# Values and gate products of two batches moved to other slots, and the causal mask of some maxima moved from VectorE to TensorE

## The reference

```python
qkv = (x @ w_qkv).reshape(b, s, 3, HEADS, HEAD_DIM)
q, k, v = (qkv[:, :, 0], qkv[:, :, 1], qkv[:, :, 2]); q = q / scale
scores = jnp.where(causal_mask, einsum('bqhd,bkhd->bhqk', q, k), NEG)
x = layernorm(x + einsum('bhqk,bkhd->bqhd', softmax(scores), v).reshape(b, s, HIDDEN) @ w_out)
weights, experts = top_k(softmax(x @ gate), 4); weights = weights / weights.sum(-1)
y = sum over the 4 experts of weight * (u * silu(g)) @ down,  with g, u = split(x @ gate_up)
out = layernorm(x + y)
```

## Time and profile before

| | before |
|---|---|
| median of 3 runs | 429.66 us (426.7 to 431.03) |
| the profiled execution: its time, its span | 431.4 us, 429.4 us |
| mean granted clock of PE | 0.964 of 2.4 GHz |
| busy over the span | PE 378.1, DVE 289.5, ACT 242.5, POOL 235.9 us |
| busy in pairs 14 to 16 (28.68 us) | PE 27.27, DVE 18.84 us |
| busy in pairs 17 to 21 (29.50 us) | PE 22.89, DVE 26.23 us |
| busy in pairs 25 to 28 (27.87 us) | PE 22.65, DVE 23.86 us |

### The profile page before, as it was taken

The page is one execution under the profiler, slowest core; times in us unless marked ns, Lnnn a source line. Parts: engine busy times, 40 slices in busy tenths (PEclk is TensorE's granted clock), DMA queues, the critical chain, the costliest instruction groups (busy, mean ns, idle before and its releaser), DMA issues.

```text
span 429.4 us, 10419 instructions
## 1 busy us (share of the span) xinstructions
PE 378.1 (88%) x2826; PEld 217.2 (51%) x2826; DVE 289.5 (67%) x1159; ACT 242.5 (56%) x534; POOL 235.9 (55%) x374
## 2 busy tenths in 40 slices
PE   5979899999996799877998999997999999989880
PEld 2526554445543356433354455665676777655340
DVE  1167868885499885989789759864656666544453
ACT  2431657765545586535766628654666656546942
POOL 5321245434232585625782672777777777646872
PEclk9999999999999899968899999999999999999966
DMA  4858554755563275393727463665665656338693
GB/s 132 266 194 223 181 179 140 223 136 161 156 197 87 52 233 162 99 275 78 227 73 230 148 172 87 179 178 172 189 176 154 173 172 177 104 83 326 264 382 129
DMA packets 54071, 74.77 MB, mean 174 GB/s; under 512 B 9842, under 2 KB 45308, under 8 KB 52480
## 3 DMA queue, kind: packets, MB, share of 16 engines
q1 hardware_dynamic: 46832, 56.93, 46.6%
q0 software_dynamic: 6912, 16.93, 10.7%
q10 hardware_dynamic: 272, 0.26, 0.2%
HBM read 46.33 MB, written 29.66 MB: 177 GB/s over the span
## 4 chain that ended last, share of the span: by engine, by line
PE 44%; DVE 18%; SPq 16%; issue 10%; DMA 5%; ACT 3%; POOL 3%; ACTq 0%; DVEq 0%; POOLq 0%
SPq L507 13%; PE PS L854 8%; PE PS L814 6%; PE PS L783 5%; PE PS L833 5%; PE PS L797 3%; DVE WOT L1412 3%; DVE junk L1412 3%; PE PS L690 3%; SPq L489 3%; PE PS L914 2%; PE PS L712 2%; POOL scratch_slots L1753 2%; PE PS L884 2%; PE PS L739 2%
## 5 line engine op out<-in xcount | busy, mean ns | idle before, releaser
L1125 ACT ACTIVATE PT<-PS 128x512 f32<-128x512 f32 x160 | 92.0, 596 | 51.5 <-PE PS L833 47.0
L1762 POOL DMA_INDIRECT scratch_y<-Y,XG x80 | 79.8, 997 | 34.0 <-issue 18.0
L1734 POOL TENSOR_SCALAR_AFFINE_SELECT PT<-PT 128x256 f32<-128x256 f32 (+1 forms) x140 | 50.2, 367 | 77.2 <-ACT PT L1125 75.9
L1753 POOL DMA_INDIRECT scratch_slots<-XP,RI x64 | 64.0, 1000 | 40.7 <-DVE XP L1354 20.6
L814 PE MATMUL PS<-KS,QS 96*128 96x512 bf16 (+3 forms) x256 | 63.7, 310 | 19.0 <-DVE MX L1412 18.3
L1412 DVE CUSTOM_DVE_ANT_0 junk<-PS,mneg 128x512 bf16<-128x512 f32 (+3 forms) x128 | 58.4, 483 | 22.3 <-PE PS L814 22.2
L833 PE MATMUL PS<-QS,KS 98*128 98x512 bf16 (+3 forms) x256 | 63.0, 308 | 1.2 <-ACT PT L1125 0.9
L690 PE MATMUL PS<-W,XGT 128*64 x320 | 60.5, 332 | 1.1 <-DVE WG L1275 0.6
L692 PE MATMUL PS<-WG,XGT 128*64 128x192 f32 x320 | 60.6, 332 | 0.0
L1412 DVE CUSTOM_DVE_ANT_0 WOT<-PS,mneg 128x512 bf16<-128x512 f32 (+3 forms) x96 | 43.9, 484 | 9.0 <-PE PS L814 9.0
L814 PEld LDWEIGHTS PS<-KS,QS 96*128 96x128 bf16 x256 | 21.7, 100 | 55.4 <-DVE MX L1412 43.8
(11 more groups left out here) (233 smaller groups left out, 658.1 us busy)
## 6 DMA issues: line engine op xcount, KB each, us to landing
XG<-scratch_slots SPq DMA_DIRECT2D x160, 65.0 KB, 2.6
scratch_qk<-PA SPq DMA_DIRECT2D x14, 384.0 KB, 3.1
W<-in_gate_up_dram SPq DMA_DIRECT2D x16, 288.0 KB, 3.7
KS<-scratch_qk SPq DMA_DIRECT2D x32, 128.0 KB, 3.8
YL<-scratch_y SPq DMA_DIRECT2D x8, 512.0 KB, 6.6
QS<-scratch_qk SPq DMA_DIRECT2D x8, 384.0 KB, 4.1
QS<-scratch_qk SPq DMA_DIRECT2D x24, 128.0 KB, 3.9
W<-in_down_dram SPq DMA_DIRECT2D x8, 288.0 KB, 4.8
```

The lines of the kernel that those rows point to most:

```text
L1125: e.activation(PT[:, p % NPT, n, :], PS[:, 2 + (rank[u] - 1) % 2, :], ACT.Exp).then_inc(st_exp, 1)
L1734: e.affine_select(out=d, in_=d, compare_op=ALU.is_ge, fill=0.0, base=0, pattern=[[0, 1 if n < 2 else 2], [1, 128]], channel_multiplier=-1) ...
L1753: e.indirect_dma_start(out=XS[:, :], out_offset=bass.IndirectOffsetOnAxis(ap=RI[:, b % 2, TOPK * q + n:TOPK * q + n + 1], axis=0), in_=XP[ ...
L1762: e.indirect_dma_start(out=YK[:, :], out_offset=bass.IndirectOffsetOnAxis(ap=XG[:, j % NXG, D + 1:D + 2].bitcast(I32), axis=0), in_=Y[:, j ...
```

## The change

`v` and `xg` of batch 2 move from slots 70 to 74 to slots 85 to 90, `v` and `xg` of batch 3 from slots 110 to 114 to 126 to 131. The last two `qk` of batch 3 move from slots 74 and 77 to 98 and 102, so that `load` 7, which reads what they make, is still behind them. `att` and `proj` of batch 0 then come one to four slots earlier. The weights of experts 6 to 14 move from slots 120 to 130 to slots 134 to 140, behind the `xg` that they wait for. Second, PE masks by a product (L828 of the changed kernel) in unit 4 of all 32 pairs, and in all five units of pairs 17 to 21 and 24 to 27; there DVE takes the maximum by `tensor_reduce`, in unit 4 by one instruction for both heads.

```diff
-WEIGHTS = ((0, 3, 75), (3, 3, 80), (6, 3, 120), (9, 3, 125), (12, 3, 130), (15, 4, 142), (19, 3, 145), (22, 3, 160),
+WEIGHTS = ((0, 3, 75), (3, 3, 80), (6, 3, 134), (9, 3, 137), (12, 3, 140), (15, 4, 143), (19, 3, 145), (22, 3, 160),
            (25, 3, 163), (28, 4, 165))
...
+VALUES_AT = (85, 126)
+VECTOR_FULL = (*range(17, 22), *range(24, 28))
...
             for c in range(2 if b > 1 else 0):
-                put(5 * (8 * b - 2) + 2 * c, ("v", b, c))
+                put(VALUES_AT[b - 2] + 2 * c, ("v", b, c))
...
             for n, m in enumerate((0, 2, 1, 3) if b > 1 else ()):
-                put(first + 4 * n + 5, ("qk", b, m))
+                put(98 + 4 * n - 8 if b == B - 1 and n >= 2 else first + 4 * n + 5, ("qk", b, m))
...
     for b in range(1, B):
-        put(5 * (8 * b - 2) + 4, ("xg", b))
+        put(5 * (8 * b - 2) + 4 if b == 1 else VALUES_AT[b - 2] + 5, ("xg", b))
...
+def mask_by_product(i, n):
+
+    return n == 4 or i in VECTOR_FULL
...
                         t = e.matmul(PS[:, kk, c0:c0 + w], QS[r][0:96, h, 128 * qt:128 * qt + 128],
-                                     KS[r][0:96, h, 0:w], start=(c0 == 0), stop=True, skip_group_check=True)
+                                     KS[r][0:96, h, 0:w], start=(c0 == 0), stop=not mask_by_product(i, n),
+                                     skip_group_check=True)
+                    if mask_by_product(i, n):
+                        wait_const(e, "idb")
+                        last = PS[:, kk, :].rearrange("p (a c) -> p a c", c=128)
+                        last = last[:, 3:4, :] if n < 2 else (last[:, 2:4, :] if n < 4 else last[:, 1:4:2, :])
+                        t = e.matmul(last, idb[:, :], mneg[:, S - 128:S].unsqueeze(1).broadcast_to(last.shape),
+                                     start=False, stop=True, skip_group_check=True)
...
-                    for h, qt, c0 in pair_scores(n, h0, 3, 2, 1):
+                    if n == 4:
+                        t = e.tensor_reduce(M[:, h0:h0 + 2, 1], PS[:, kk, :].rearrange("p (h n) -> p h n", h=2),
+                                            AX.X, ALU.max)
+                    for h, qt, c0 in pair_scores(n, h0, 3, 2, 1) if n < 4 else ():
                         w = 128 * (qt + 1)
-                        t = e.tensor_tensor_reduce(sums_of(i, kk)[:, c0:c0 + w], PS[:, kk, c0:c0 + w], mneg[:, S - w:S],
-                                                   1.0, LOWEST, ALU.add, ALU.max, M[:, h, qt:qt + 1])
+                        if mask_by_product(i, n):
+                            t = e.tensor_reduce(M[:, h, qt:qt + 1], PS[:, kk, c0:c0 + w], AX.X, ALU.max)
+                        else:
+                            t = e.tensor_tensor_reduce(sums_of(i, kk)[:, c0:c0 + w], PS[:, kk, c0:c0 + w],
+                                                       mneg[:, S - w:S], 1.0, LOWEST, ALU.add, ALU.max,
+                                                       M[:, h, qt:qt + 1])
```

## The result

The changed kernel took 422.5 us in the median of its four runs (422.1 to 425.5), the kernel before 428.7 (426.7 to 431.0); the ratio is 0.9848, 95% interval [0.9801, 0.9894], about 6 us. The profiled execution took 422.5 us, its span is 420.8; that of before took 431.4, its span 429.4.

What follows compares the result with a forecast made beforehand. PE was taken to bound pairs 14 to 16 and 22, DVE 17 to 21 and 25 to 28. Terms -8.9 - 4.9 + 4.8 + 0.3 + 0.3 = -8.4 us gave 421.3 us for the median, range 414.5 to 428.5.

Steps and rivals of the forecast that it cites:

- What bounds: In the maxima, PE bounds pairs 14 to 16 and 22, DVE bounds pairs 17 to 21 and 25 to 28.
- the 8.9 us in pairs 14 to 16: Two halves of `v`, one `xg` and two `qk` leave these PE-bound pairs, and all their time comes back: -8.9 us.
- Pair 22: Batch 3's `v` and `xg`, 5.47 us, leave it; it ends at 4.5 us, a gain of 4.9.
- floor of the quiet pairs: Pairs 8 to 11 take 4.43 us each, the least a pair was taken to need.
- The cover: PE's idle time hides moved work: 4.6 of 6.61 us in pairs 17 to 21, 3.6 of 5.22 in 25 to 28.
- The rival that blocks don't fit: Moved blocks on PE let DVE run dry and cost full length in both routing stretches: +7.1 us, 436.8; 11 in 100.
- The masks: PE pays 0.44 us per fully masked pair, 2.2 in pairs 17 to 21; DVE gains 0.07 per unit 4.
- The clock: Time at 1.2 GHz given back once PE is full: 1.7 us in pairs 17 to 21, 3.4 in 25 to 28.
- Behind the maxima: What follows the maxima is untouched and moves with their end: 0 us.
- the chances: Faster than 425.4 us: 0.52 from the main case, 0.09 full gain, half of 0.22 for POOL and weights, given as 0.71.
- POOL: POOL becomes the bound in pairs 19 to 22 and 27 to 31, making `pv` wait: +4 us, 425; 14 in 100.
- The backlog of the weights: Weights of experts 6 to 14 delay the maxima's small transfers, needed in pair 30: +3 us, 424; 8 in 100.

Runs made afterwards that it cites:

- b_again1: The kernel before, unchanged, profiled a second time; 431.1 us in one run.
- e6_batch2: The kernel before with only the moves of batch 2's `v` and `xg` and batch 3's last two `qk`, all masks on DVE; 425.3 us, ratio to before 0.9882.
- e9_halves: The changed kernel with only unit 4's masks on PE and each moved half of `v` cut in two pieces, one slot between; 422.7 us, ratio to before 0.9846.
- e10_moves_again: The changed kernel's new order with no mask on PE, all masks on DVE, run a second time; 422.0 us, ratio to before 0.9822.
- e5_batch3: The kernel before with only the moves of batch 3's `v` and `xg` and the weights behind them, all masks on DVE; 424.9 us, ratio to before 0.9899.
- e2_masks: The changed kernel with the order put back to that of before, so only the masks change; 428.7 us, ratio to before 1.0022.
- e4_fused_dve: The changed kernel, but DVE keeps the fused masked operation in units 0 to 3 of the nine fully masked pairs; 423.9 us, ratio to before 0.9888.
- e1_moves: The changed kernel's new order with all masks left on DVE, none on PE; 423.2 us, ratio to before 0.988.
- e8_weights_late: The changed kernel with the weights of experts 6 to 21 put later still, slots 143 to 158 instead of 134 to 145; 423.4 us, ratio to before 0.985.

## Why the prediction was right, and where its terms were not

**What bounds** was read rightly: PE in pairs 14 to 16 and 22, DVE in 17 to 21 and 25 to 28. In the first two nearly all the work taken out came back. Of the 8.9 us in pairs 14 to 16, 0.7 stayed: the shorter stretch has a wait of PE for DVE of 1.0 us, now that DVE has 17.90 us of work in 20.44. Pair 22 stopped at 4.90, 0.5 above the floor of the quiet pairs.

**The cover** was larger than forecast. I let 4.6 of 6.6 us of idle time in pairs 17 to 21 serve; with moves and masks 5.3 of 6.4 us of waits went, and the 1.4 us that PE is idle now are 0.3 a pair, between the 0.4 that I took off and the 0.2 of the quiet pairs. The moves alone cost 4.1 us there (b_again1 against e6_batch2), so 4.8 of their 8.9 were covered. The rival that blocks don't fit is refuted by that, and by the 1.1 us of waits left; e9_halves says that the length of a piece doesn't matter in pairs 17 to 21.

**The masks** were priced at 2.2 us for pairs 17 to 21. By the difference to e10_moves_again they cost 32.77 - 32.09 = 0.7, by doubling them 1.05. The step that failed is the one that took PE's time for a mask as the stretch's, though PE has waits into which part of it falls: I had filled the cover with the moved work and left none for the masks. That the plain reduction is no dearer than the fused one held: 0.598 against 0.611 us, while the Trainium skill ("VectorE: DVE Perf Modes", "Rules for kernel authors") calls `tensor_reduce` the slowest operation of DVE; no run here bears that out for a maximum over PSUM. Unit 4's gain is 0.09 where I had 0.07.

**The clock** was about right in size and wrong as a gain. I took 5.1 us as given back. Of the forecast for pairs 17 to 21 that is 1.7, and the first and second profile of before differ by 1.55 there: right in size, but the stretch was not there in the second profile, so it is no gain over a usual run.

For pairs 25 to 28 I reckoned half of each low microsecond as lost and one stretch of two as given back, 3.4 us. Between before and e6_batch2, the same order there with 13.7 and 3.4 us of low clock, lie 2.2 us: 0.22 per low microsecond, and not 0.5. That DVE bounds there and PE had room would explain it, but no run takes this apart, and in pairs 17 to 21, where DVE bounds too, the 3.4 us cost 0.46 each. Both stretches were gone, which by 0.22 is 3.0 us: two errors that nearly cancel, so the clock doesn't explain why the difference was -1.5 us and not +0.3. The rest does. Moves less cover and masks were to add 5.5 + 1.8 - 3.6 = 3.7 us; from the 24.9 that the old order would take by this estimate without a low clock, the changed kernel's 26.38 is 1.5 more. Of that the moves alone are 0.8 (e5_batch3), and the masks, which cost nothing there in the old order (24.18 in e2_masks), the other 0.7. So here too moved work and masks were priced too high, not the clock.

**Behind the maxima** I had nothing, and 2.2 us went. PE waits there for tiles of rows from memory in both kernels (the bracket: idle before it, and for what), in the changed one

```profile
284.51 0.41 PE L665 MATMUL PS<-idf,XG 128*128 128x128 f32 x2 [1.71 <-DMA XG<-scratch_slots]
285.85 0.69 PE L665 MATMUL PS<-idf,XG 128*128 128x128 f32 x2 [0.92 <-DMA XG<-scratch_slots]
```

and in the one before

```profile
295.77 0.41 PE L658 MATMUL PS<-idf,XG 128*128 128x128 f32 x2 [1.64 <-DMA XG<-scratch_slots]
296.92 0.43 PE L658 MATMUL PS<-idf,XG 128*128 128x128 f32 x2 [0.74 <-DMA XG<-scratch_slots]
```

but in the changed kernel the clock then fell for 6.8 us:

```profile
285.30:292.10 6.80, 6.25 (x32) 4.09 (x33) 2.16 (x5) 1.51 (x5) 5.28 (x6) 0.50 0.65 205
```

and in the one before it didn't. From the first product of round 9 to that of round 12 are 15.2 us with that and 12.3 without. It isn't the change's: b_again1, the old kernel, has 6.8 us of it at 294.1 and needs 14.9 us for the same rounds, while e4_fused_dve, the new order without such a stretch there, needs 12.5.

So the sum, -8.4 us against 431.4, met 422.5 within 0.5 us with errors that cancelled: costs in pairs 17 to 21 and 25 to 28 that I put 3.3 us too high, gains in pairs 14 to 16 and 22 that I put 1.1 too high, and 2.2 us behind the maxima that I had not. The honest size of the change is the ratio, 6 us, of which e1_moves and e10_moves_again show the moves to be all. The forecast of the median, made by the whole difference from the median then known, was 1.2 us too low: the two profiled executions differ by 8.9 us, the medians by 6.2, since that of before was 2.7 us over its median. Of the chances, a slip that changes nothing: 0.52 + 0.09 + 0.11 is 0.72, not 0.71.

**The other rivals.** POOL ran from 137.9 to 157.6 us without a pause, and the waits of PE show none for it; that its lag was covered by the pair between mask and use is argued, no run took it away. The backlog of the weights cost nothing in the changed kernel, as e8_weights_late shows, but it is no empty rival: its sign, PE waiting at L847 for the maxima, came in one of nine profiles with the weights in the new slots, e4_fused_dve, at 1.75 us. How often it comes is open.

## What to carry to other kernels

When two engines take turns as the bound, move work of the one into stretches of the other and count what waits it meets there; most of PE's idle time could be used here (5.3 of 6.4 us), even by pieces of 1.83 us, three times as long as one reduction. Whatever else is added to that stretch shares the same waits. Before counting the clock as a gain, take a second profile of the old kernel: a stretch at the lower level was worth 0.2 to 0.5 us for each of its microseconds here, and it may not be there next time. An edit that relieves the engine that bounded before is worth nothing, or costs, once other work has made the other engine the bound.

## What the runs showed that I had not expected

- The same instructions at the same clock repeat to 0.01 us: pairs 17 to 21 took 32.77, 32.77 and 32.76 us in the changed kernel, its second profile and e8_weights_late. What differs between profiles of the new order is where a stretch at 1.2 GHz falls, and the part behind the maxima, 201.5 to 205.9 us.
- Products on PE that compute nothing new went with a higher granted clock: in the old order 17.1 and 6.8 us at 1.2 GHz in pairs 14 to 31 without masks, none with them (e2_masks). One or two profiles are little, and e9_halves had 6.8 us with unit 4's masks; whether the masks are the cause stays open.
- A fused reduction of 512 with the read of the accumulator behind it takes 0.013 us more distance than a plain one, though the profile books 0.08 us for the read.
